# Three of sixteen scan inputs built by ScalarE and TensorE, and nine C products on GpSimd

## What is computed

```
dt = clip(sigmoid(u @ dt_w.T + dt_b), 1e-4, 1)
Bm = u @ B_w.T ; Cm = u @ C_w.T
def step(state, inp):                  # 16 states per channel
    dA = exp(clip(dtt[:, :, None] * A, -5, 5))
    dB = dtt[:, :, None] * bt[:, None, :] * ut[:, :, None]
    state = dA * state + dB + 1e-06
    y = sum(state * ct[:, None, :], axis=-1) + D * ut
    return (state, y)
```

## Time and profile before

| | us |
|---|---|
| median of 3 runs | 2840.7 (2837.89 to 2843.85) |
| the profiled execution | 2837.7 |
| its span, first to last instruction | 2836.0 |
| its mean granted TensorE clock | 0.959 of full |

### The profile page before, as it was taken

The page is one execution under the profiler, slowest core; times in us unless marked ns, Lnnn a source line. Parts: engine busy times, 40 slices in busy tenths (PEclk is TensorE's granted clock), DMA queues, the critical chain, the costliest instruction groups (busy, mean ns, idle before and its releaser), DMA issues.

```text
span 2836.0 us, 48476 instructions
## 1 busy us (share of the span) xinstructions
PE 2510.6 (89%) x15232; PEld 2197.7 (77%) x15232; DVE 2228.4 (79%) x4890; ACT 2029.6 (72%) x4675; POOL 2234.2 (79%) x1354
## 2 busy tenths in 40 slices
PE   7788898888888888988898888889887699999998
PEld 4787777777777778877887777788776588888887
DVE  2999999999999999999999999999996233333332
ACT  2988888888888888888888888888884133333332
POOL 1999999999999999999999999999994133333333
PEclk9899999999999999999999999999996899999999
DMA  4222222223222222222222322232220588888886
GB/s 177 76 82 88 79 80 87 79 80 105 87 83 83 94 79 87 87 79 80 87 80 85 107 79 83 85 93 80 87 80 15 160 199 201 202 200 199 201 200 152
DMA packets 138181, 309.62 MB, mean 109 GB/s; under 512 B 15040, under 2 KB 79680, under 8 KB 137792
## 3 DMA queue, kind: packets, MB, share of 16 engines
q1 hardware_dynamic: 110848, 270.03, 30.9%
q0 software_dynamic: 27072, 36.46, 6.3%
HBM read 258.42 MB, written 48.01 MB: 108 GB/s over the span
## 4 chain that ended last, share of the span: by engine, by line
DVE 37%; PE 34%; ACT 14%; issue 10%; DMA 1%; POOL 1%; DVEq 0%; SPq 0%; POOLq 0%; ACTq 0%
DVE bank L1247 14%; PE bank L667 13%; DVE room L1247 9%; PE bank L685 8%; DVE room L1256 7%; ACT room L798 6%; ACT bank L814 5%; PE bank L552 5%; PE bank L600 2%; PE bank L616 2%; PE bank L530 2%; ACT bank L856 1%; PE bank L589 1%; DVE zs L1222 1%; DVE hid L1326 1%
## 5 line engine op out<-in xcount | busy, mean ns | idle before, releaser
L1036 POOL TENSOR_TENSOR room<-dtu,b_all 128x1024 f32<-128x1024 f32 x512 | 1203.5, 2373 | 17.7 <-DVE dtu L1424 13.8
L798 ACT ACTIVATE room<-room,neg_a 128x256 f32<-128x256 f32 x2048 | 868.0, 497 | 0.8 <-DVE room L1213 0.8
L814 ACT ACTIVATE bank<-room,eps_col 128x512 f32<-128x512 f32 x1024 | 695.0, 682 | 235.6 <-DVE carry L1261 164.0
L600 PE MATMUL bank<-ident,room 128*128 128x128 f32 x4096 | 554.4, 283 | 168.7 <-POOL room L1025 88.6
L600 PEld LDWEIGHTS bank<-ident,room 128*128 128x128 f32 x4096 | 481.5, 146 | 224.2 <-POOL room L1025 98.0
L1247 DVE TENSOR_TENSOR_SCAN bank<-room,carry,bank 128x256 f32<-128x256 f32 x864 | 577.4, 733 | 20.8 <-ACT bank L814 20.8
L1025 POOL TENSOR_TENSOR room<-room,c_all 128x1024 f32<-128x1024 f32 x224 | 531.9, 2374 | 29.4 <-issue 17.4
L1161 POOL DMA_INDIRECT out<-room,ids x144 | 223.8, 1554 | 409.2 <-DMA out<-room,ids 205.8
L1326 DVE SCALAR_TENSOR_TENSOR hid<-hid,bank 128x256 f32<-128x256 f32 (+1 forms) x312 | 129.9, 416 | 420.8 <-ACT hid L909 420.8
L1247 DVE TENSOR_TENSOR_SCAN room<-room,carry,bank 128x256 f32<-128x256 f32 x672 | 447.9, 725 | 10.9 <-ACT bank L814 10.3
L552 PE MATMUL bank<-xnT,w_conv 128*128 128x256 f32 x3072 | 404.5, 288 | 7.0 <-ACT xnT L837 5.5
(11 more groups left out here) (150 smaller groups left out, 2939.4 us busy)
## 6 DMA issues: line engine op xcount, KB each, us to landing
b_all<-b_scratch SPq DMA_DIRECT2D x128, 512.0 KB, 4.0
c_all<-b_scratch SPq DMA_DIRECT2D x128, 512.0 KB, 5.0
room<-in_wgu SPq DMA_DIRECT2D x72, 704.0 KB, 5.8
room<-in_wd SPq DMA_DIRECT2D x72, 384.0 KB, 3.6
room<-x_by_expert SPq DMA_DIRECT2D x72, 260.0 KB, 2.9
x_in<-in_x SPq DMA_DIRECT2D x32, 256.0 KB, 5.8
x<-in_x SPq DMA_DIRECT2D x32, 256.0 KB, 2.7
out<-x SPq DMA_DIRECT2D x32, 256.0 KB, 4.2
```

The lines of the kernel that those rows point to most:

```text
L600: last = mm(tr_bank[k][:, b * P:(b + 1) * P], v[n % VRING][:, b, k * P:(k + 1) * P], ident[:, :], is_transpose=True, start=False, stop=(n ...
L798: last = af(da[n % RING][:, b, :], dt[c.par][:, b, :], ACT.Exp, scale=neg_a[:, b, n:n + 1])
L814: af(v_slot(c, n, h)[:, :], v[n % VRING][:, 2 * h:2 * h + 2, :].rearrange("p b t -> p (b t)"), ACT.Identity, bias=eps_col[:, 0:1]).then_in ...
L1036: nc.gpsimd.tensor_tensor(out=v[n % VRING][:, :, :], in0=dtu[:, :, :], in1=row, op=ALU.mult) \
```

## The change

The inputs of states 11, 13 and 15 no longer come from GpSimd and ScalarE's bank copy. dtu is transposed once a chunk by TensorE into `pr_bank[1]` and copied by ScalarE to `dtuT` (token on the partition): the first half at the end of the step before, the second in slot 0. B of these states comes to `b_tok` with one small load for each 128 tokens, where it is a column. ScalarE computes dtuT x B + 1e-6 for a state three slots ahead (`b_times_turned`), TensorE transposes it into the scan's bank in the slot of the state itself, its first half at the slot's head, its second behind the slot's state transposes and projection (`turn_state`), and the scan waits for `turn_ready`. GpSimd makes the C products of 7 and 9 as well. `hid` shrinks to one chunk; the expert stage keeps its hid in the room of the scan. `second_weight` goes from slot 15 to 14.

```diff
-BY_POOL = [0, 2, 4, 6, 8, 10, 12]
+BY_POOL = [0, 2, 4, 6, 7, 8, 9, 10, 12]
+TURNED = [11, 13, 15]
...
+        dtuT = sb("dtuT", [P, NT, DI])
+        b_tok = [sb(f"b_tok{i}", [P, NT, len(TURNED)]) for i in range(2)]
...
-        hid = sb("hid", [P, THRING, TC])
+        hid = sb("hid", [P, HB, TC])
...
# SP
+            def load_b_tok(c):
+                sp_wait(b_written, c.index * 16 + 16)
+                sp_wait(tok_ready, inputs(c.plus(-1), 0)[1])
+                for k in range(NT):
+                    src = b_scratch[c.par, TURNED[0]:NS:2, k * P:(k + 1) * P].rearrange("n t -> t n")
+                    sp.dma_start(b_tok[c.par][:, k, :], src, allow_slow_non_contiguous=True)                       .then_inc(b_tok_loaded, 16)
...
             def load_b(c, p):
-                sp_wait(v_mul, c.index * NS + NEAR * (p - 1))
+                sp_wait(v_mul, inputs(c, NEAR * (p - 1))[0] if p else inputs(c.plus(-1), NS - NEAR)[0])
...
                         write_b(proj)
+                        load_b_tok(proj)
                         load_b(proj, 0)
...
# TensorE
+            def turn_dtu(c, k, post):
+                pe.wait_ge(dtu_ready, c.index + 1)
+                pe.wait_ge(zs_done, (c.index + 1) * NT)
+                if post:
+                    pe.wait_ge(h_ready, units_out(post, 1))
+                wait(pe, dtuT_ready, c.index * NT + k)
+                transposes(pr_bank[1], [dtu[:, b, k * P:(k + 1) * P] for b in range(KD)]).then_inc(dtu_turned, 1)
...
+            def turn_state(c, n, h):
+                pe.wait_ge(tok_ready, inputs(c, n + 1)[1])
+                bank_free(*before(c, n, h))
+                for j in range(2):
+                    for k in range(NT):
+                        b = 2 * h + j
+                        last = nc.tensor.transpose(v_slot(c, n, h)[:, j * TC + k * P:j * TC + (k + 1) * P],
+                                                   v_tok[n % VRING][:, k, b * P:(b + 1) * P], ident[:, :])
+                last.then_inc(turn_ready, 1)
...
                 def __call__(self, scan, post, proj, norm):
                     for slot in range(NS):
+                        if scan and slot in TURNED:
+                            turn_state(scan, slot, 0)
                         if slot == 0 and post:
                             state_transpose(post, NS - 2)
                             state_transpose(post, NS - 1)
+                        if slot == 0 and scan and post:
+                            turn_dtu(scan, 1, late_of(post))
...
                         if norm and slot == 13:
                             proj_norm(norm)
+                        if scan and slot in TURNED:
+                            turn_state(scan, slot, 1)
+                        if proj and slot == 15:
+                            turn_dtu(proj, 0, post)
                         if post:
                             for u in units_of(slot, GU_SLOT):
...
# ScalarE
+            def take_dtu(c, k):
+                act.wait_ge(dtu_turned, c.index * NT + k + 1)
+                af(dtuT[:, k, :], pr_bank[1][:, :], ACT.Copy).then_inc(dtuT_ready, 1)
+
+            def b_times_turned(c, n):
+                act.wait_ge(dtuT_ready, c.index * NT + NT)
+                act.wait_ge(b_tok_loaded, (c.index + 1) * NT * 16)
+                act.wait_ge(tr_ready, c.index * NS + n - VRING + 1)
+                i = turned_inputs(n)
+                for k in range(NT):
+                    af(v_tok[n % VRING][:, k, :], dtuT[:, k, :], ACT.Identity, scale=b_tok[c.par][:, k, i:i + 1],
+                       bias=eps_col[:, 0:1]).then_inc(tok_ready, 1)
...
                         c, n = ahead(slot + 1)
-                        if c:
+                        if c and n not in TURNED:
                             add_eps(c, n, 1)
+                        if scan and post and slot == 0:
+                            take_dtu(scan, 1)
...
                         c, n = ahead(slot + 2)
-                        if c:
+                        if c and n not in TURNED:
                             add_eps(c, n, 0)
+                        if scan and slot + 3 in TURNED:
+                            b_times_turned(scan, slot + 3)
+                        if proj and slot == 15:
+                            take_dtu(proj, 0)
...
# GpSimd
+                        if post and slot == 14:
+                            second_weight(post)
                         if post and slot == 15:
-                            second_weight(post)
                             scatter(post, 1)
                         n = slot + MUL_LEAD
-                        if scan and n < NS:
+                        if scan and n < NS and n not in TURNED:
                             b_times_dtu(scan, n)
...
# VectorE
                 for h in range(2):
-                    dve.wait_ge(v_ready, halves(c, n) + h + 1)
+                    if n in TURNED:
+                        dve.wait_ge(turn_ready, inputs(c, n)[1] + h + 1)
+                    else:
+                        dve.wait_ge(v_ready, inputs(c, n)[0] * 2 + h + 1)
```

More of the change, by code:

```diff
@@ L90, in dve_products, with turned_inputs, pool_inputs @@
     return n - pool_products(n)
+def turned_inputs(n):
+    return sum(1 for m in TURNED if m < n)
+def pool_inputs(n):
+    return n - turned_inputs(n)
 def units_of(slot, slots):
@@ L163, in build @@
         v = [room[:, i, :, :] for i in range(VRING)]
+        v_tok = [room[:, i, :, :].rearrange("p b t -> p (b t)").rearrange("p (k d) -> p k d", k=NT) for i in range(VRING)]
         da = [room[:, VRING + i, :, :] for i in range(RING)]
@@ L199, in build @@
         tab_zero = sb("tab_zero", [P, EXPERTS], I32)
-        parts = [("t_gu", KM, 2 * HID), ("t_dn", HB, DM), ("xt", NT, ROW), ("xtT", KM, TILE), ("yt", NT, DM)]
+        parts = [("t_gu", KM, 2 * HID), ("t_dn", HB, DM), ("xt", NT, ROW), ("xtT", KM, TILE), ("yt", NT, DM),
+                 ("t_hid", HB, TC)]
         assert max(2 * sum(k * n for _, k, n in parts), KD * (TAPS * DI + DM) + KM * DI) <= (VRING + RING + 2) * KD * TC
@@ L213, in build @@
                         .rearrange("p (t e) -> p t e", t=TILES) for i in range(2))
-        t_gu, t_dn, xt, xtT, yt = (views[name] for name, _, _ in parts)
+        t_gu, t_dn, xt, xtT, yt, t_hid = (views[name] for name, _, _ in parts)
         raw_z = late[:, KD * (TAPS * DI + DM):KD * (TAPS * DI + DM) + KM * DI].rearrange("p (k i) -> p k i", k=KM)
@@ L273, in build @@
         v_ready = sem("v_ready")
+        b_tok_loaded = sem("b_tok_loaded")
+        dtu_turned = sem("dtu_turned")
+        dtuT_ready = sem("dtuT_ready")
+        tok_ready = sem("tok_ready")
+        turn_ready = sem("turn_ready")
         clip_done = sem("clip_done")
@@ L341, in before, with hid_tile @@
             return None if k < 0 else (Chunk(0, 0).plus(k // (2 * NS)), k // 2 % NS, k % 2)
-        def hid_slot(c, u):
-            return (u + c.par * UNITS) % THRING
+        def hid_tile(c, u, tiled):
+            return t_hid[c.par][:, u, :] if tiled else hid[:, u, :]
         def run(body):
@@ L543, in proj_conv @@
                 if half == 0 and j == 0:
+                    wait(pe, dtuT_ready, c.index * NT)
                     wait(pe, h_ready, units_out(c.plus(-3), 1))
@@ L602, in state_transpose, with bank_free @@
                 last.then_inc(tr_ready, 1)
+            def turn_dtu(c, k, post):
[5 more added lines that the diff above has]
+                transposes(pr_bank[1], [dtu[:, b, k * P:(k + 1) * P] for b in range(KD)]).then_inc(dtu_turned, 1)
+            def bank_free(c, n, h):
+                if n in BY_POOL:
+                    pe.wait_ge(half_ready, halves(c, n) + h + 1)
+                elif c.pos != 3:
+                    pe.wait_ge(dve_kept, kept(c, n)[1] + h + 1)
+                else:
+                    pe.wait_ge(dve_product, products(c, n)[1] + h + 1)
+            def turn_state(c, n, h):
[7 more added lines that the diff above has]
+                last.then_inc(turn_ready, 1)
             def post_y(c, h):
@@ L685, in down @@
                         last = mm(dn_bank(tiled)[:, k * DM:(k + 1) * DM],
-                                  hid[0:rows, hid_slot(c, m), k * P:(k + 1) * P], w[0:rows, m, :],
+                                  hid_tile(c, m, tiled)[0:rows, k * P:(k + 1) * P], w[0:rows, m, :],
                                   start=(m == 0), stop=(m == HB - 1))
@@ L907, in gate @@
                 act.wait_ge(gu_ready, c.index * UNITS + u + 1)
-                act.wait_ge(dn_ready, c.index + HEAD)
-                af(hid[0:rows, hid_slot(c, u), :], bank[0:rows, 0:TC], ACT.Tanh, scale=0.5).then_inc(th_ready, 1)
+                act.wait_ge(dn_ready, c.index + HEAD + (0 if tiled else 1))
+                af(hid_tile(c, u, tiled)[0:rows, :], bank[0:rows, 0:TC], ACT.Tanh, scale=0.5).then_inc(th_ready, 1)
             class Body(Phases):
@@ L939, in start @@
                     decays(Chunk(0, 0), 2)
+                    for k in range(NT):
```

(6 more changed lines are left out.)

8 lines of the change are left out of this document (7 added, 1 removed).

## The result

The changed kernel takes 3027.3 us (3025.8 to 3028.3, 4 runs) against 2839.5: ratio 1.066, 95% interval 1.065 to 1.068. The forecast was 2982, range 2895 to 3035; the kernel got 188 us slower where 141 were forecast. The profiled execution has a span of 3024.1 us.

A forecast was written before the change was run, and what follows sets the result against it. VectorE looked like the bound; a new loop through TensorE's stretch and state 11 would pace each chunk. 4.2 + 0.5 (clock) = 4.7 us in 30 chunks, 141 us on 2840.7, gives 2982; range 2895 to 3035.

The forecast's parts named there:

- TensorE's long stretch: TensorE from state 15's transposes (slot 0) to those of state 9 (slot 11): 46.23 us, busy for 44.63.
- the forecast's own range: Range of the main forecast alone, 2935 to 3015 us, with chance 0.6.
- The loop: State 11's scan waits for TensorE until 46.9 us, then VectorE needs 21.4: 68.3 a chunk against 66.1.
- the sum: Chunk from 66.1 to 69.95 us, plus 0.7 in every second chunk: on average 4.2 more, before the clock.
- The slow start that the sum let go: Half clock at state 15's transposes mostly goes, as the idle time before them shrinks to 1.6 us: -0.6.
- State 13: Its turns stand behind TensorE's other work, so VectorE stalls 1.25 us for the first half, 0.4 for the second.
- VectorE's 3.1 us: Saved a chunk by moving products 7 and 9 to GpSimd; lies ahead of state 11, where VectorE will wait.
- Net +0.5: Clock term a chunk: +1.1 for a fall in slot 11, -0.6 for the slow start before state 15.
- The fall in slot 11: TensorE idle 3.1 us instead of 1.82, then half clock in 7 chunks of 10 at 1.6 us: +1.1.
- ScalarE, the loads, the expert stage: ScalarE's added 1.8 us a chunk hidden; b_tok loads, at most 8 us each, cost about nothing; expert stage unchanged.
- Faster, as TensorE has room: Rival, chance 0.05: slot 11 comes before VectorE wants it, cycle falls by some 2 us, 2779 us.
- everything slips: Rival, chance 0.15: low clock in each chunk, and state 13's second half or ScalarE's queue shows: 6.7 x 30, 3041 us.

The follow-up runs named there:

- experiment 6: Changed kernel plus matmuls of zeros in three TensorE gaps (twelve in slot 11, ten ahead of unit 2, eight ahead of state 15's transposes): 2962.5 us.
- experiment 8: Changed kernel with only state 11 turned and only product 7 added to GpSimd: 2946.5 us, ratio 1.038 to the kernel before.
- 9: Changed kernel with only state 15 turned and only product 7 added to GpSimd: 2872.2 us, ratio 1.011 to the kernel before.
- Experiment 3: Changed kernel with both turns of state 13 put ahead of gate_up of unit 1: 2964.4 us.
- experiment 1: Changed kernel with the C products of 7 and 9 left on VectorE, so the turned inputs alone: 3026.6 us.
- experiment 5 with twelve: Changed kernel plus twelve matmuls of zeros in TensorE's gap of slot 11: 2978.6 us (with twenty, 3023.8 us).
- experiment 10: Changed kernel with states 13 and 15 turned, 11 not, and both turns of 13 ahead of gate_up of unit 1: 2883.4 us, ratio 1.015.
- experiments 2: Kernel before with the C products of 7 and 9 moved to GpSimd and no turned inputs: 2951.0 us, ratio 1.039.
- 11: Changed kernel with only state 15 turned and product 11 moved to GpSimd in place of 7: 2937.6 us, ratio 1.035.

## Why the prediction held, and which terms were off

The forecast of slower, by a loop through TensorE's long stretch and states 11 and 13, came true, and for its reason. The time is inside the wide range, but outside the forecast's own range of 2935 to 3015, and the rise is 188 us for 141; the clock is what is missing.

**The loop: right, its size in part by luck.** TensorE's start at state 15 to the scan of state 11 was put at 46.9 us, with 0.7 more in every second chunk; it was 46.9 to 47.4 in eight chunks. But the sum was one for full clock, and at full clock, in experiment 6, it is 46.2 to 46.9, 46.6 on average for 47.25. The slow start that the sum let go filled the difference. Then follows VectorE's own time of 21 us, unchanged. Experiments 8 and 9 show that the place behind the long stretch costs, not the amount of work: 74 us lie between them.

**State 13: right in mechanism and, at full clock, in size.** 1.25 + 0.4 were worked out; experiment 6 has 1.31 + 0.26. Experiment 3 shows that the order of TensorE's list is the cause.

**VectorE's 3.1 us worth nothing: right,** by experiment 1 directly.

**Without the clock the sum was right, in part by luck:** 2840.7 + 30 x 4.2 = 2967, and experiment 6, whose clock stays at full speed through the chunks from 134 to 2233 us, measured 2962.5. Two errors cancel in it: the sum took a chunk from 66.1 to 70.3 us, where experiment 6 has 69.4 and the kernel before 65.5. Also, the kernel before has slow starts that experiment 6 does not have.

**The clock: mis-sized.** It was the term "Net +0.5" a chunk, 15 us; between the changed kernel and experiment 6 lie 65 us, 2.1 a chunk. Two parts of it were off. The fall in slot 11 had a chance of 7 in 10 at 1.6 us; the 1.6 was right (unit 0 took 1.56 us longer in the chunk shown, and experiment 5 with twelve gave back 49 us, 1.6 a chunk), but it came in every one of eight chunks, 0.5 a chunk more. And I let the slow start at state 15's transposes go (-0.6), where it came in six of eight chunks and had been in two of four; between the changed kernel and experiment 6 the scan of state 11 moves by 0.5 us on average. The last rested on TensorE's idle time there shrinking to 1.6 us; it is 1.9 to 2.1 with 0.9 before dtu's transposes. What decides there was not tried apart. The kernel before has slow starts of its own, so 65 us are not all due to the change; no run keeps its clock up, so what they cost it is not shown.

**ScalarE, the loads, the expert stage: right.** The turned product is 0.755 us for 0.72, the loads land in 2.2 us within a bound of 8. From the last y_tok product to the end of the span it is 667 us for 669. ScalarE's added work became visible only where the wait for TensorE at state 11 was gone (experiment 10, and likely 9).

**The rivals.** "Faster, as TensorE has room" fell with the first window: TensorE had no room in its long part. The Trainium skill, Perfetto Trace Analysis, Identifying the Most-Contended Engine, judges TensorE by the weight loads' busy share, beside its share of the peak. That busy time is 236 of 300 us both before and after, so in this case it does not show that TensorE has come to hold VectorE; the order of the lists does. The case "everything slips" (3041) is the nearest to the number, by its first half, a low clock in each chunk; the second, ScalarE's queue, was not in it.

## What to carry to other kernels

Where an engine works off its list in strict order, look for the stretch in which it has no gap and ask where its next result is wanted: work that is new for others at the end of that stretch closes a loop, whatever the average share says, while relief ahead of the new wait is worth nothing. A new gap of some 3 us on TensorE should be priced with a half clock behind it: gaps of 3.0 to 3.2 us were followed by it in each of eight chunks of the changed kernel. It is not certain: in experiment 8 unit 0 ran at full clock (1.99 us) behind a gap of 3.22 us in one of the four kinds of chunk. A gain in TensorE's length can be eaten by a slow stretch that moves: the same cut gave 2 us with the clock free and 20 with it kept up. Before a product is moved to an engine that is 96% busy, follow when each of its results is wanted: here every such move without the three turned inputs (experiments 2, 8, 9 and 11) came back as a wait on TensorE.

## What was not expected of the hardware

A few matmuls of zeros in TensorE's gaps keep the granted clock at 1.00 over 300 us and bring 65 us of 3027 in this kernel, although they add 25 us in 300 to its busy time. An f32 matmul of 128 columns is two passes of 0.11 us each (forty passes for twenty in 4.46 us), a transpose one (eight in 0.87 us). The slow stretches were regular: in the changed kernel one lay behind the gap of slot 11 in each of eight chunks and one at the head of the long stretch in six of them, and with z shortened the second came in all eight.
